# One gated delta-rule layer on one core: the last token of each chunk read from the state behind the chunk, three lag targets in place of four, y kept in time order

## The reference

```python
def step(S, inp):                              # S: 8 x 8 for each sequence and head
    k_t, q_t, v_t, beta_t, a_t = inp
    S = S * a_t[..., None, None]
    kv_mem = jnp.einsum('bhd,bhde->bhe', k_t, S)
    delta = (v_t - kv_mem) * beta_t
    S = S + k_t[..., :, None] * delta[..., None, :]
    y_t = jnp.einsum('bhd,bhde->bhe', q_t, S)
    return (S, y_t)
...
ctx = _rmsnorm(ys, norm_w) * jax.nn.silu(gate)
x = _layernorm(x + ctx @ Wo.T + bo)
x = _layernorm(x + expert_of(x))
```

## Time and profile before

| what | value |
|---|---|
| median of 3 executions | 808.16 us (805.93 to 808.61) |
| the profiled execution | 808.61 us, span from first to last instruction 808.6 us |
| busy: TensorE, VectorE, GpSimd, ScalarE | 689.3, 630.6, 642.0, 414.5 us |
| one chunk on VectorE, its seven instructions (mean) | 0.689, 0.382, 0.732, 0.418, 0.426, 0.690, 0.827 us |
| the chain's windows | from 26.8 us to about 569 us |
| from there to the end | 240 us: last outputs, routing, experts |

### The profile page before, as it was taken

How to read it: one execution, slowest core, us unless ns; L and a number is a source line. 1 busy time by engine, 2 the same in 40 slices (tenths; PEclk the granted TensorE clock), 3 DMA queues, 4 the chain that set the end, 5 groups by cost and what they waited for, 6 DMA issues and landing times.

```text
span 808.6 us, 13837 instructions
## 1 busy us (share of the span) xinstructions
PE 689.3 (85%) x3545; PEld 516.8 (64%) x3545; DVE 630.6 (78%) x1697; ACT 414.5 (51%) x1281; POOL 642.0 (79%) x789
## 2 busy tenths in 40 slices
PE   8679788998999989899899995977775769999991
PEld 3436465566756657566575564756665769999890
DVE  3899999999999999999999999899611524666430
ACT  6635555457564575645656455232231245666561
POOL 2989999899999999999999999987537334444574
PEclk9989999999999999999999997878677789999996
DMA  6823234333343332443333422064433355767630
GB/s 171 206 75 94 82 103 115 87 81 98 94 116 102 82 97 80 110 121 82 89 88 110 109 69 82 17 199 143 158 109 116 119 170 184 244 231 235 224 109 8
DMA packets 135918, 97.27 MB, mean 120 GB/s; under 512 B 95630, under 2 KB 110225, under 8 KB 135714
## 3 DMA queue, kind: packets, MB, share of 16 engines
q1 hardware_dynamic: 130514, 87.55, 36.7%
q0 software_dynamic: 4320, 8.43, 3.2%
q10 hardware_dynamic: 1008, 0.43, 0.2%
HBM read 39.80 MB, written 31.43 MB: 88 GB/s over the span
## 4 chain that ended last, share of the span: by engine, by line
DVE 36%; PE 34%; POOL 13%; issue 5%; ACT 4%; another core or an unknown queue 4%; SPq 1%; DMA 1%; POOLq 0%; DVEq 0%; ACTq 0%
PE banks L433 10%; PE banks L689 7%; DVE banks L1852 6%; DVE upd L1840 6%; DVE banks L1826 5%; PE banks L446 5%; DVE prod L1810 4%; POOL q_prod L1290 4%; DVE banks L1836 4%; DVE mix L1830 4%; DVE upd L1821 3%; PE banks L742 2%; POOL u L1290 2%; PE banks L674 1%
## 5 line engine op out<-in xcount | busy, mean ns | idle before, releaser
L1290 POOL TENSOR_TENSOR q_prod<-s_keep,q_gam 128x512 f32<-128x512 f32 x128 | 139.9, 1097 | 12.8 <-ACT s_keep L1000 11.8
L742 PE MATMUL banks<-q_prod,ident 128*128 128x256 f32 x496 | 119.6, 397 | 23.8 <-POOL q_prod L1290 23.6
L1000 ACT ACTIVATE s_keep<-banks 128x128 f32<-128x128 f32 x128 | 49.8, 389 | 158.5 <-DVE upd L1840 158.5
L742 PEld LDWEIGHTS banks<-q_prod,ident 128*128 128x128 f32 x496 | 96.1, 199 | 49.0 <-POOL q_prod L1290 35.7
L433 PE MATMUL banks<-xs_t,w_tile 128*128 128x128 f32 x852 | 114.1, 284 | 13.0 <-ACT xs_t L463 5.2
L542 POOL DMA_INDIRECT out<-rows_out,xs x71 | 70.0, 986 | 59.7 <-ACT rows_out L523 53.2
L433 PEld LDWEIGHTS banks<-xs_t,w_tile 128*128 128x128 f32 x852 | 106.0, 199 | 16.4 <-issue 9.3
L1852 DVE TENSOR_REDUCE banks<-upd 128x128 f32<-128x640 f32 x127 | 105.1, 827 | 7.6 <-DVE upd L1840 0.5
L577 DVE TENSOR_TENSOR hid<-banks,silu 128x384 f32<-128x384 f32 x71 | 39.6, 558 | 89.6 <-PE banks L433 36.3
L689 PE MATMUL banks<-kkqk,ident 128*128 128x320 f32 (+2 forms) x272 | 88.6, 488 | 9.9 <-ACT y_rms L1028 5.3
L1826 DVE TENSOR_REDUCE banks<-prod 128x64 f32<-128x576 f32 x128 | 93.7, 732 | 0.0
(11 more groups left out here) (219 smaller groups left out, 1459.9 us busy)
## 6 DMA issues: line engine op xcount, KB each, us to landing
w_tile<-gate_up_we SPq DMA_DIRECT2D x71, 352.0 KB
xs<-x_sorted SPq DMA_DIRECT2D x71, 64.5 KB
x_ct<-in_x_ct SPq DMA_DIRECT2D x16, 256.0 KB, 3.0
k_dram<-kq_s SPq DMA_DIRECT2D x16, 256.0 KB, 3.0
q_dram<-kq_s SPq DMA_DIRECT2D x16, 256.0 KB, 3.7
out<-v_s SPq DMA_DIRECT2D x16, 256.0 KB, 2.7
out<-beta SPq DMA_DIRECT2D x16, 256.0 KB, 2.6
k_h<-k_dram SPq DMA_DIRECT2D x16, 256.0 KB
```

Of the source, the lines that this page charges most:

```text
L742: i = mm(out, ident[:, :], q_prod[m][:, :, d, :], start=(m == 0 and d == 0), stop=(d == DH - 1), skip_group_check=True)
L1290: b.step(label, win, lambda: tt(out, x, y, op))
```

## The change

- The output of the last token of a chunk is q of that token times the state *behind* the chunk, with no decay and no lag term. So `q_gam` of chunk c+1 holds in its slot 0 the raw q of the last token of chunk c (copied by ScalarE, new `q_ends`: `q_raw` and `q_next`), and in slots 1 to 3 the decayed q of tokens 0 to 2 of its own chunk. `q_prod` keeps its 512 elements a chunk.
- The lag terms then have three targets: lags 0 to 2 with 3, 2 and 1 tokens. `query_key`, `qkd` and `y_lags` lose the 512-element product of lag 0 with four targets (and become 384, 256 and 128 elements), `lag_sums` 64 of 320 columns, `y_deltas` 4, 3, 2, 1 tokens to 3, 2, 1.
- The last token of a window has its product in chunk 0 of the next window, so VectorE sums it (`y_next`, a reduce of 128 elements to 16 into y's bank) in chunk 2, slot 3; in the last window in chunk 1, slot 3. It waits for `q_prod0` of this window and for y of the window before. `y_square` waits for it and moves behind chunk 2's copies.
- `y_sums` moves from ahead of `count` and `lag_sums` to behind the norm sums of k, into the bank of q; the root moves behind the root of k. The first `y_n` part moves from chunk 3 slot 3 to chunk 4 slot 3, and the last from chunk 5 slot 3 to chunk 7 slot 1 (not in the last window). `y_store` waits for that last part.
- y is in time order (c, j), so `project_gate` and `context` have contiguous operands, while `y_deltas` writes with a stride of four.
- The last chunk also computes its state, and `last_outputs` begins with `y_ends` and `y_next`.

```diff
-        q_prod = two_a("q_prod", [P, 4, DH, DH * 2 * C])
+        q_prod = two_a("q_prod", [P, DH, DH * 2, T // 2])
...
 def y_chunks(win, m):
-                out = y_ps[win % 2].rearrange("p (n c) -> p c n", c=NCH)[:, 4 * m:4 * m + 4, :]
+                out = y_slots(win)[:, :, 0:T // 2 - 1] if m == 0 else y_slots(win)[:, :, T // 2 - 1:T - 1]
...
-                        i = mm(out, ident[:, :], q_prod[m][:, :, d, :], start=(m == 0 and d == 0),
+                        i = mm(out, ident[:, :], q_prod[m][:, d, :, 1 - m:], start=(m == 0 and d == 0),
...
 def y_deltas():
-                    for d in range(C):
-                        size = (C - d) * NCH
-                        i = mm(y[:, :, d * NCH:], ident[:, :], y_prod[:, at:at + DH * 2 * size], start=False, stop=True,
+                    for d in range(C - 1):
+                        size = (C - 1 - d) * NCH
+                        i = mm(y[:, :, d:C - 1, :], ident[:, :], y_prod[:, at:at + DH * 2 * size], start=False, stop=True,
...
 tensor engine, tail:
+                b.wait(dve, "y_next", p)
                 late_chunks("y1_7", 7, 8)
...
 tensor engine, window:
-            if b.post:
-                b.wait(dve, "qkd3", n - 1)
-                b.wait(act, "v_s", a)
-                y_sums(p, pre_ps[:, 2, 0:2 * T])
             if b.route:
                 count(w - 3)
             if b.pre:
...
-                lag_sums("kkqk", n, pre_ps[:, 2, :], 0, 320)
+                lag_sums("kkqk", n, pre_ps[:, 2, :], 0, 256)
             if b.load:
                 b.wait(act, "kq_s", a)
                 k_norms(pre_ps[:, 0, :], a)
+            if b.post:
+                b.wait(act, "kq_s", min(a, NW - 1))
+                y_sums(p, pre_ps[:, 1, 0:2 * T])
...
 scalar engine:
+            def q_ends(win):
+                b.wait(pool, "q_prod7", win - 2)
+                b.step("q_raw", win, lambda: A(q_gam[win % 2][:, 1:NCH, :, :, 0].rearrange("p c d b -> p d b c"),
+                                               q_h[win % 2][:, :, :, C - 1, 0:NCH - 1], ACT.Copy))
+                to = q_gam[(win + 1) % 2][:, 0, :, :, 0] if win < NW - 1 else q_end[:, :, :]
+                b.wait(pool, "q_prod0", win - 1)
+                b.step("q_next", win, lambda: A(to, q_h[win % 2][:, :, :, C - 1, NCH - 1], ACT.Copy))
...
             keep(NCH * w + 3)
...
+            if b.post:
+                y_root()
             keep(NCH * w + 4)
...
             if b.pre:
+                q_ends(n)
                 solve_ends(n)
...
 vector engine:
+            def y_next_part():
+                b.wait(pool, "q_prod0", w)
+                b.wait(pe, "y", p)
+                b.step("y_next", p, lambda: v.tensor_reduce(
+                    y_ps[p % 2].rearrange("p (n t) -> p n t", t=T)[:, :, T - 1],
+                    q_prod[0][:, :, :, 0].rearrange("p d n -> p n d"), AX, ALU.add))
...
+                if b.post and c == 2 and k == 3:
+                    y_next_part()
...
                 if b.post and c == 4 and 3 <= k:
-                    y_n_part(k - 1)
+                    if k == 3:
+                        b.wait(act, "y_r1", p)
+                    y_n_part(k - 3)
                 if b.post and c == 5 and k < 4:
-                    y_n_part(k + 4)
+                    y_n_part(k + 2)
...
+                if b.post and c == 6 and k == 3:
+                    y_n_part(6)
+                if b.post and c == 7 and k == 1:
+                    y_n_part(7)
 last_between:
+                if c == 1 and k == 3:
+                    y_next_part()
 last_outputs:
-                    e.wait_ge(s_delta, NN)
+                    e.wait_ge(s_state, NN)
+                b.wait(act, "q_next", NW - 1)
+                b.step("y_ends", ...)
+                b.wait(pe, "y1_6", NW - 1)
+                b.step("y_next", ...)
```

More of the change, by code:

```diff
@@ L844, in late_chunks @@
             def late_chunks(label, first, last):
-                out = y_ps[w % 2 if b.last else p % 2].rearrange("p (n c) -> p c n", c=NCH)[:, first:last, :]
+                out = y_slots(w if b.last else p)[:, :, C * first - 1:C * last - 1]
                 def go():
                     for d in range(DH):
-                        i = mm(out, ident[:, :], q_prod[1][:, first - 4:last - 4, d, :], start=False,
+                        i = mm(out, ident[:, :], q_prod[1][:, d, :, C * first - T // 2:C * last - T // 2], start=False,
                                stop=(d == DH - 1), skip_group_check=True)
@@ L870, in pe_body @@
                 b.wait(act, "kq_s", NW - 1)
+                b.wait(act, "y_r0", p - 1)
                 count(w - 3)
@@ L942, in pe_body @@
                 y_chunks(p, 1)
-                b.wait(pool, "y_prod3", p)
+                b.wait(pool, "y_prod2", p)
                 y_deltas()
@@ L1162, in start_up @@
                 q_squares(0)
+                q_ends(0)
                 solve_ends(0)
@@ L1297, in q_times_s @@
                     b.wait(pe, f"y{c // 4}", win - 1)
+                if c == 0:
+                    b.wait(dve, "y_next", win - 2)
+                    b.wait(act, "q_next", win - 1)
+                if c == 1:
+                    b.wait(act, "q_raw", win)
                 shape = [P, DH, DH, 2, C]
@@ L1650, in first_queries @@
                 if k == 0:
-                    b.step("q_norm", 0, lambda: v.tensor_scalar(q_norm[0][:, :], ps[:, 256:320], DH * DH * RMS_EPS, None,
-                                                                ALU.mult))
-                    b.step("qkd0", 0, lambda: v.tensor_copy(qkd[0][:, 0:64], ps[:, 96:160]))
-                else:
-                    at, dk0 = lag_at[k], decays[0]
-                    by0 = (a_h[0][:, :, 1:4, :], dk0[:, :, 4:7:2, :], dk0[:, :, 5:6, :])
-                    b.step(f"qkd{k}", 0, lambda: v.tensor_tensor(lag(qkd[0], at + 64, k), lag(ps, at + 160, k), by0[k - 1],
-                                                                 ALU.mult))
+                    q_norm_part(0)
+                qkd_part(k, 0)
             def early(c):
-                if b.post and c == 3:
+                if b.post and c == (3 if b.last else 4):
                     b.wait_dma(s_yst, p)
@@ L1675, in between @@
                     return
-                if w == 0 and c == 2 and k < 4:
+                if w == 0 and c == 2 and k < 3:
                     first_queries(k)
@@ L1689, in between @@
                     route_part(r, 9)
-                if b.post and c == 3 and 3 <= k:
-                    if k == 3:
-                        b.wait(act, "y_r1", p)
-                    y_n_part(k - 3)
+                if b.post and c == 2 and k == 3:
+                    y_next_part()
                 if b.pre and c == 4 and k < 3:
@@ L1746, in last_outputs @@
                 if not b.dry:
-                    e.wait_ge(s_delta, NN)
+                    e.wait_ge(s_state, NN)
+                b.wait(act, "q_next", NW - 1)
+                ends = mix[:, :, :, :].rearrange("p n i j -> p n (i j)")[:, :, 0:DH]
+                b.step("y_ends", p, lambda: v.tensor_tensor(
+                    ends.rearrange("p (e b) d -> p e b d", b=2),
+                    chain_ps[0][:, 0:P].rearrange("p (e b d) -> p e b d", e=DH, b=2),
+                    q_end[:, :, :].rearrange("p d b -> p b d").unsqueeze(1).to_broadcast([P, DH, 2, DH]), ALU.mult))
+                b.wait(dve, "y_ends", p)
+                b.wait(pe, "y1_6", NW - 1)
+                b.step("y_next", p, lambda: v.tensor_reduce(
+                    y_ps[p % 2].rearrange("p (n t) -> p n t", t=T)[:, :, T - 1], ends, AX, ALU.add))
+                if not b.dry:
                     for k in range(11, n_table_a):
@@ L1837, in chunk @@
                 between(c, 2)
-                if live and g < NN - 1:
+                if live:
                     e.wait_ge(s_delta, g + 1)
```

119 lines of the change are left out of this document (64 added, 55 removed).

## The result

The changed kernel takes 812.72 us (median of 6 executions, 810.91 to 815.02), the kernel before 806.79 in the same comparison (803.31 to 808.61). The ratio is **1.0065**, 95% interval 1.0038 to 1.0093: slower, by 5 to 6 us. The forecast was 805.1, that is 3.1 us less than before, with the largest chance on "faster". The time lies in the range from 801 to 815; the direction was wrong.

A forecast was written before the change was run, and what follows sets the result against it. VectorE was taken to bound the windows, with 7.3 us of waits on top. Terms of -1.0 in the windows and -2.1 behind them gave -3.1, from 808.61 to 805.5, as a median 805.1; 8-in-10 range 801 to 815.

The forecast's parts named there:

- The lag sums end in time: Windows 3 to 10 and 14: lag sums end before `kkd` wants them, so its wait goes, -4.9 and -2.4 us.
- I take +0.5: First `y_n` part, chunk 4 slot 3: root ready at +19.8, just when wanted; +0.5 us for all windows together.
- first rival: Also rival 1: wait moves to the root, 1.5 us in each of 8 windows, +12.0, giving 817.1; chance 0.2.
- `y_next` at 0.05 a window: VectorE's added 128-number reduce costs 0.05 us in each of 14 windows, +0.7 us.
- GpSimd, SyncE and k's way: Window turn: `y_store` at -2.0, `k_load` at +1.4, GpSimd waits 2 us for k; hidden, worth nothing on the path.
- Window 15 at +5.1: Later `y_store` makes `y_next` wait 6.0 us in chunk 1 of window 15, swallowing chunk 3's `count` wait; net +5.1.
- The tail at -2.1: Behind the windows, `y_deltas` took 5.18 us and keeps 0.6 of its columns: -2.1 us.
- well ahead: Last chunk's extra state, 2.6 us of VectorE, ends at about 572, before the last late chunk and `y_deltas` at 579.72.
- Rival 3: Gain ends in the tail: later y of window 14, or `y_deltas`' 2.1 us not reaching the end; 807.5, chance 0.15.
- forecast -1.0: Sum up to window 14's last `y_n`: -4.9 - 2.4 + 0.5 + 0.7 + 5.1 = -1.0 us.

The follow-up runs named there:

- b0: The kernel before, unaltered, run again on the experiments' chips: 781.11 us, ratio 1.0011.
- e13: The kernel before with filler matmuls in window 15 alone, none ahead of `count` in the windows: 779.28 us, ratio 0.9972 to the kernel before.
- e3: The kernel before with only its last `y_n` part moved from chunk 5 slot 3 to chunk 7 slot 1: 783.03 us, ratio 1.0047.
- e11: The kernel before with filler matmuls in the windows and window 15, and k and q loaded ahead of y's store and load: 776.97 us, ratio 0.9949.
- e0: The changed kernel, unaltered, run again on the experiments' chips: 786.18 us, ratio 1.0077 to the kernel before.
- e4: The changed kernel with two unread 512-column matmuls ahead of `count` in windows 3 to 14: 782.36 us, ratio 1.0033 to the kernel before.
- e5: The changed kernel with k's store and the k and q loads ahead of y's store and load on SyncE's queue: 782.15 us, ratio 1.0029.
- e1: The changed kernel with window 14's last `y_n` parts back in chunk 5, so its y store is early: 781.19 us, ratio 1.0009.
- e8: The changed kernel with the edits of e1, e4 and e5, and VectorE's pads ahead of `y_ends` and `y_next`: 776.25 us, ratio 0.9960.
- e9: e8 with three fillers ahead of window 15's residual, six ahead of its output projection and three ahead of `y1_6`: 774.17 us, ratio 0.9938.
- e10: The changed kernel with the edits of e1 and e4 alone: 778.10 us, ratio 0.9989 to the kernel before.
- e12: e9 run once more, unaltered: 774.58 us, ratio 0.9922 to the kernel before.

## Why the prediction was wrong

**The lag sums end in time: right, and less than it seemed.** No `kkd` waits in any changed kernel. The 7.3 us of the earlier trace rows were gained in the first profile. In b0 the same waits are 5.7 us, partly in other windows. e13 loses those of windows 5 to 13 by the draw alone, and e3 and e11 have few without the change.

**"I take +0.5" for a margin of nil: wrong.** This step failed first. It rests on lag sums of 5.0 us, eight tenths of one row that held a slow stretch, and on the sentence that the slow stretch is thereby inside. For a stretch of that length it was: where the lag sums take 5.0 to 5.4, nothing waits. What it left out is the window in which the low level covers the end of `count` as well and nearly all of the lag sums. In window 7 `count` takes 1.42, the lag sums 6.62, they end at +18.3, not +16.3, and the first `y_n` part waits 1.64. Measured: 3.2 us of root waits in the first profile (windows 3 and 7), 6.5 in e0 (four windows), where 0.5 was put into the sum. In window 3 the lag sums also started late, at +13.2, behind a late `one_hot`.

It is the mechanism of the first rival, which had 1.5 us a window and said that the sign turns at 2.1 windows. I gave it 0.2 because one slow row seemed to bound the others. I put a second slow stretch on the norm and square sums; it was one longer stretch, on `count` and the lag sums. And the rule that I quoted, the Trainium skill ("TensorE: Matmul & The Clock Gate", Part 1: The HAM clock gate), spoke for this case. e4 agrees with it: with two more matmuls the granted clock on the lag sums of window 6 is 1.00, and in windows 4 to 13 they all take 3.70.

**`y_next` at 0.05 a window**: 0.085, from windows of 33.51 in place of 33.42. +1.2 in place of +0.7. The row of 136 on one partition took 0.28; the 128 in strided groups took 0.37.

**GpSimd, SyncE and k's way: nearly right.** -2.07 and +1.30 were forecast as -2.0 and +1.4; k was there 4.1 us behind its issue, for 3.4, and the wait of 2.0 is 2.6. `count` still begins when `one_hot` is ready, at +10.0. What I missed is ScalarE: the copies of a chunk stand behind the square of q, and the reduce of VectorE in windows 2 and 3 waited 1.1 us for `d_keep`. e5 removes this. It is small and only early.

**Window 15 at +5.1: right.** The wait is 5.97 (forecast 6.0) and seven chunks are 5.3 longer. e1 shows that it is this store. It is the largest cost of the change, and it was in the forecast in full. e0 has 4.55 in place of 5.97: TensorE's half of `y_chunks` took 3.97 there and 5.57 in the first profile.

**The tail at -2.1: not seen where it was expected.** `y_deltas` shrank as told: 2.88 at the low level, 1.31 in window 15 where 2.17 times 0.6 gives 1.30. (The Trainium skill, "SBUF — State Buffer", Door 1: The DMA port swizzle, expects non-contiguous PSUM access to cost; with a stride of four this row shows no price.) The square of y starts level with before. But SyncE's 12 loads now start at 578.51 and not at 571.70, since the pads stand behind `y_next`, which waits for a late chunk. I had said that the extra state ends "well ahead" of `y_deltas` and had not asked who waits for what follows it on VectorE. In e0 this held y's last store for 2.4 us. In the first profile the root itself starts 5.2 us behind the end of the square sums, and in that of before 2.3; the releaser isn't in the trace, and these 2.9 us stay open. There y's last store goes out 3.3 us later than before (595.25 for 591.91), so at that point nothing of the 2.1 is left. Rival 3 was this case in kind.

**The sum.** From chunk 0 of window 0 to the last chunk, in the first pair of profiles: -7.3 for the waits of `kkd`, -0.4 in window 0, +1.3 for `y_next`, +4.5 in windows 2, 3 and 7 (3.2 for the root, 1.1 for `d_keep`, the rest at chunk 0 of window 3), +5.3 in window 15, together +3.4; measured +3.5 (542.97 for 539.51), forecast -1.0. Behind the windows that pair gives 1.8 back, but behind y's last store, where executions differ by up to 4 us in any case. This execution of the changed kernel is one of its shorter ones, so the pair differs by less than the medians. On the experiments' chips the windows are 7.2 longer (e0 against b0) and nothing comes back behind them, and the medians differ by 5.6. So of the miss of some 8 us, the root's step makes 3 to 6, `y_next` and `d_keep` about 1.6. The tail's share is 2 at most, and no time here shows it. That the measured time lies in the range owes most to the width that rival 1 gave it.

## What to carry to other kernels

One row with a slow stretch in it doesn't bound the next one: take the row at each clock level from several iterations, and give the slowest to the margin that is thinnest. Work taken off TensorE ahead of a wait can leave it idle, and what follows may be slower for it. Here two dummy matmuls took away the root waits, 6.5 us in e0, nearly as much as the fifth of the columns had saved (7.3). Where the slow stretches come by the draw, one profile of each kernel can show a gain that the edit didn't make, so compare an edited kernel with several profiles of the unedited one. When an instruction is moved on an engine, follow also what now stands behind it, its engine's next steps and the queue that waits for them, and look at the last iterations apart: the store that was free in 13 windows cost 5 us in the 14th.

## What the runs showed of the hardware that was not expected

- The same work in the same place takes three kinds of time in the changed kernels without filler (windows 4 to 13): 3.70 us, 5.0 to 5.4 or 6.3 to 6.7 for 16 matmuls of 256 columns. The granted clock is 1.00 in the first kind (window 6) and 0.50 in the slow stretches of the others (windows 11 and 7). For 320 columns it is 4.55 or 6.1 to 6.24 in windows 3 to 13.
- Idle time of 1.1 to 1.9 us ahead of `count` came with all three kinds, idle time under 0.5 us with the fast kind alone (14 of 14); with filler in that place (e4, e8, e9, e10, e12) windows 4 to 13 had no wait at all.
- No time at the low level is twice the 3.70 or the 4.55, so that level covers a part of it; 320 columns (6.24 at most in windows 3 to 13) even took less than the slowest 256 columns (6.29 to 6.69).
- The kernel before takes 807 us in the first comparison and 780 in the experiments, with windows of the same length (33.42 and 33.43). The difference lies behind the windows: 242 us to the end of the span in the one, 213 in b0. From 600 to 680 us TensorE is busy for 57.2 us in the one and 70.8 in the other. That the chip makes the difference isn't shown.
